# Chunk output of a selective scan: a seventh drive of sixteen by ScalarE and TensorE, the scaled input added by a diagonal matmul, the chunk written by ScalarE

## The reference

```
chunks = xn.reshape(B, L, 4, 64)...            # 4 chunks per batch item
h  = exp(dt*A[s]) * h + (dt*x)*B[s]            # for each of 16 states s, over 1024 tokens
y  = sum over s of h*C[s]  +  xc*D_param
ym = out_proj_w @ (y * silu(z))                # 128 -> 64 channels
ym = ym + skip_scale * chunks                  # what is called the skip below
```

## Time and profile before

| | us |
|---|---|
| median of 3 runs | 1836.05 (1835.17 to 1837.93) |
| the profiled execution | 1832.81 |
| its span, first to last instruction | 1830.9 |
| scans of the second item, gate of chunk 0 to the last read | 433.9 to 575.7 |
| mixture of experts, from | 1252.2 |

### The profile page before, as it was taken

One profiled execution on the slowest core, in us unless ns is written; L12 is line 12 of the kernel. 1 busy time (PEld: TensorE's weight loads), 2 busy tenths in 40 slices (PEclk: granted clock), 3 DMA queues, 4 the chain that ended last, 5 costly groups with the idle time before them and its releaser, 6 DMA issues. The chain is left out here.

```text
span 1830.9 us, 22984 instructions
## 1 busy us (share of the span) xinstructions
PE 1564.3 (85%) x6577; PEld 1012.4 (55%) x6578; DVE 1158.7 (63%) x1344; ACT 1002.1 (55%) x1950; POOL 1074.1 (59%) x574
## 2 busy tenths in 40 slices
PE   5589889979888888888898888673599999999997
PEld 2144435644444553443564444452488888888896
DVE  3399998489997579998758999746522222222222
ACT  6768775878874887885687877321122222222222
POOL 0499991279995158999037999300345555455543
PEclk9799999999999999999998999895699999999999
DMA  3356650156762055765026676642022222222222
GB/s 104 99 185 228 221 197 10 50 184 224 241 203 86 1 170 196 248 204 169 2 78 217 195 240 200 247 179 71 25 36 34 37 37 39 35 34 40 34 33 26
DMA packets 78401, 222.43 MB, mean 121 GB/s; under 512 B 12588, under 2 KB 31349, under 8 KB 74966
## 3 DMA queue, kind: packets, MB, share of 16 engines
q1 hardware_dynamic: 62390, 202.54, 32.8%
q0 software_dynamic: 15904, 18.66, 6.6%
HBM read 199.76 MB, written 19.82 MB: 120 GB/s over the span
## 5 line engine op out<-in xcount | busy, mean ns | idle before, releaser
L474 PE MATMUL psum<-HC_sb,ident_sb 128*128 128x512 f32 x768 | 368.4, 606 | 36.1 <-POOL HC_sb L1257 25.5
L1986 ACT ACTIVATE hgt_sb<-psum_moe,b_sb 128x256 f32<-128x256 f32 (+1 forms) x312 | 116.5, 456 | 379.8 <-PE psum_moe L1893 252.0
L474 PE MATMUL psum<-experts_sb 64*128 64x512 f32 (+5 forms) x834 | 258.4, 551 | 70.6 <-DVE HC_sb L1577 18.8
L1893 PE MATMUL psum_moe<-XGT_sb,w1s_sb 128*128 128x256 f32 (+1 forms) x1248 | 254.9, 363 | 0.0
L2138 DVE TENSOR_TENSOR YS_sb<-psum_moe,b_sb 128x256 f32<-128x256 f32 x71 | 30.1, 424 | 352.8 <-PE psum_moe L1893 349.2
L1893 PE MATMUL psum_moe<-experts_sb,hgt_sb 128*128 x1136 | 251.7, 379 | 0.7 <-DVE YS_sb L2138 0.7
L1870 POOL DMA_INDIRECT out<-YS_sb,scat_sb x71 | 128.3, 1806 | 209.5 <-DVE YS_sb L2142 193.1
L1138 ACT ACTIVATE psum<-experts_sb 128x1024 f32<-128x1024 f32 x168 | 186.1, 1108 | 118.2 <-DVE experts_sb L1567 70.5
L474 PEld LDWEIGHTS psum<-HC_sb,ident_sb 128*128 128x128 f32 x768 | 139.8, 191 | 189.3 <-issue 104.6
L1160 ACT ACTIVATE experts_sb<-experts_sb 128x128 f32<-128x128 f32 x704 | 227.7, 388 | 18.4 <-PE psum L477 15.2
L1893 PEld LDWEIGHTS psum_moe<-XGT_sb,w1s_sb 128*128 128x128 f32 x1248 | 219.5, 192 | 25.5
(11 more groups left out here) (298 smaller groups left out, 2381.0 us busy)
## 6 DMA issues: line engine op xcount, KB each, us to landing
X_XT_sb<-bc_rows SPq DMA_DIRECT2D x116, 512.0 KB, 4.1
DA_sb<-bc_rows SPq DMA_DIRECT2D x88, 512.0 KB, 5.2
experts_sb<-bc_rows SPq DMA_DIRECT2D x40, 512.0 KB, 5.4
SQ_sb<-bc_rows SPq DMA_DIRECT2D x40, 512.0 KB, 5.9
T_sb<-bc_rows SPq DMA_DIRECT2D x20, 512.0 KB, 5.5
experts_sb<-w1T SPq DMA_DIRECT2D x8, 1024.0 KB, 19.8
experts_sb<-w2T SPq DMA_DIRECT2D x8, 1024.0 KB, 21.8
X_sb<-x_tok SPq DMA_DIRECT2D x5, 1024.0 KB, 6.9
```

Source lines behind the costliest of these rows:

```text
L474: return nc.tensor.matmul(o, lhsT, rhs, start=start, stop=stop, **k)
L1893: return nc.tensor.matmul(o, lhsT, rhs, start=start, stop=stop, **k)
L1986: m = nc.scalar.activation(HGT[:, k, 4 * h + q, 0:w], psum[:, 2 * h + q // 2, (q % 2) * 2 * P:(q % 2) * 2 * P + w], ACT.Gelu, bias=b1[:, b ...
```

## The change

In the last three chunks of an item seven states instead of six are turned: 1, 4, 6, 8, 10, 12 and 14, where it was 1, 4, 6, 9, 12 and 14. So state 9 goes to GpSimd, and states 8 and 10 leave it. POOL_READS stays. For chunks 0, 1 and 2 the skip on VectorE is gone. The output projection now goes into the half of banks 4 and 5 that the C row used, half by half behind sum_states at s = 2 and s = 3, and each half gets a second matmul, which adds the scaled input by a diagonal of 64 x 64 (SKIP, made once at the start). ScalarE copies the sum to YM (chunk_out) at s = 5, behind its decay and blocks, and c_row of s = 5 waits for that. The decay of s = 3 doesn't wait for the chunk any more. The last chunk of an item is as it was.

```diff
-TURNED_DRIVES = ((6, 9, 12, 15),) + ((1, 4, 6, 9, 12, 14),) * (NC - 1)
+TURNED_DRIVES = ((6, 9, 12, 15),) + ((1, 4, 6, 8, 10, 12, 14),) * (NC - 1)
...
+        SKIP = FB[:, 0:DM]
... (TensorE, c_row)
+                    if c and s == 5:
+                        pe.wait_ge(ym_done, b * NC + c)
... (TensorE, out_proj)
-                def out_proj(c):
-                    i = min((c + 1) * NS + 1, NI - 1)
-                    pe.wait_ge(h_ready, b * NI + (i + 1))
-                    p0 = DM * (c % 2)
+                def out_proj(c, h):
+                    i, p0 = (c + 1) * NS + 1, DM * (c % 2)
+                    pe.wait_ge(yf_ready, b * NC + c + 1)
+                    pe.wait_ge(dve_read, b * dve_reads(NI) + dve_reads(i + 1))
+                    at = psum[p0:p0 + DM, 4 + h, :]
+                    mm(at, outp_w[:, :], YF[:, h * HL:(h + 1) * HL], True, False)
+                    m = mm(at, SKIP[p0:p0 + DM, :], xn[p0:p0 + DM, c // 2, h * HL:(h + 1) * HL], False, True)
+                    if h:
+                        m.then_inc(op_ready, 1)
... (TensorE, the loop over i)
-                    if i % NS == 1 and c:
-                        out_proj(c - 1)
...
                     sum_states(i - 1)
+                    if c and i % NS in (2, 3):
+                        out_proj(c - 1, i % NS - 2)
... (ScalarE, decay)
-                    if c and s == 3:
-                        act.wait_ge(ym_done, b * NC + c)
...
+                def chunk_out(c):
+                    act.wait_ge(op_ready, b * NC + c + 1)
+                    p0 = DM * (c % 2)
+                    nc.scalar.activation(halves(YM[p0:p0 + DM, c // 2, :]), crep[p0:p0 + DM, :, :], ACT.Copy).then_inc(ym_done, 1)
... (ScalarE, the loop over i)
                     scale_blocks(i)
+                    if i >= NS and i % NS == 5:
+                        chunk_out(i // NS - 1)
... (VectorE)
-                    if c and s == 2:
-                        skip(c - 1)
... (VectorE, start)
+            fold(v.tensor_tensor(SKIP, ident[:, 0:DM], ident[:, DM:P], ALU.add))
+            fold(v.tensor_scalar(SKIP, SKIP, scal[:, 0:1], None, ALU.mult))
```

More of the change, by code:

```diff
@@ L815, in sum_states, with last_out_proj @@
                     m.then_inc(ysum_done, 1)
-                def out_proj(c):
-                    i = min((c + 1) * NS + 1, NI - 1)
-                    pe.wait_ge(h_ready, b * NI + (i + 1))
-                    p0 = DM * (c % 2)
+                def out_proj(c, h):
+                    i, p0 = (c + 1) * NS + 1, DM * (c % 2)
+                    assert not on_pool(i) and all(on_pool(i + k) for k in (1, 2, 3)) and not on_pool(i + 4)
+                    pe.wait_ge(yf_ready, b * NC + c + 1)
[5 more added lines that the diff above has]
+                        m.then_inc(op_ready, 1)
+                def last_out_proj():
+                    c, p0 = NC - 1, DM * ((NC - 1) % 2)
+                    pe.wait_ge(h_ready, b * NI + NI)
                     for h in range(NH):
-                        if c == NC - 1 and h == 0:
+                        if h == 0:
                             pe.wait_ge(yf_half, b + 1)
@@ L825, in out_proj @@
                             pe.wait_ge(yf_ready, b * NC + c + 1)
[L826 to L829, removed]
+                        mm(psum[p0:p0 + DM, 2 + h, :], outp_w[:, :], YF[:, h * HL:(h + 1) * HL], True,
+                           True).then_inc(op_ready if h else op_half, 1)
                 pe.wait_ge(bc_spread, b * (3 * NC * 16) + 3 * NC * 16)
@@ L848, in scans @@
                 xhat_turn(b + 1, 0)
-                out_proj(NC - 1)
+                last_out_proj()
                 xhat_turn(b + 1, 1)
@@ L1605, in gate @@
                     v.tensor_tensor(halves(YF), ysum, halves(SZ[:, c, :]), ALU.mult).then_inc(yf_ready, 1)
[L1607 to L1612, removed]
                 for i in range(NI):
@@ L1692 @@
 PREP_EPS, PREP_DVE, PREP_ALL = 6, 11, 11 + 3 + 2 + 6 + 5 + 1
-FOLD_NBR, FOLD_WG, FOLD_DVE = 12, 14, 20
+FOLD_NBR, FOLD_WG, FOLD_DVE = 12, 14, 22
 FIRST_AT = 18
```

## The result

The changed kernel takes 1845.7 us in the median (1841.46 to 1850.34), the kernel before 1836.05. The ratio is 1.005, with a 95% interval of 1.0037 to 1.0064: slower by 9.65 us. The profiled execution is the one of 1845.7 us, with a span of 1843.9.

A forecast was written before the change was run, and what follows sets the result against it. GpSimd was taken to pace the tails, with VectorE close behind, and the output chain the heads. Heads +6.8 and tails -4.9 give +1.9 us per item, +7.6 on 1832.8, plus 3.2 to the median: 1843, range 1827 to 1857.

The forecast's parts named there:

- What bounds the kernel: GpSimd paces the tails, VectorE close behind; heads follow gate, output projection on TensorE, skip on VectorE, decay of s = 3.
- The chain in the head: From gate through TensorE's queue to ScalarE's copy at 13.3 us, then decay and scan of s = 6; heads +6.8 per item.
- The handover to TensorE: At the start of the head's chain: gate and handover to TensorE take 1.35 us.
- The changes of shape: On TensorE between gate and copy: changes of matmul shape cost 0.09 to 0.14 each, 0.5 us in the chain.
- The copy: ScalarE's copy of 64 x 1024 from PSUM, once per chunk: 1.02 us, as partitions don't count.
- The lower bound of 0.5: ScalarE's copy at 0.5 us if half the partitions were half the time; takes 6 us off, to 1837.
- The tails: From scan of s = 6 to the next gate: 0.2, 2.4 and 2.3 us come back in chunks 1 to 3, -4.9.
- that GpSimd can't run far ahead: In tails 2 and 3 GpSimd's reads wait for the late scan of s = 6, limiting work ahead; no separate size.
- The sum: Heads +6.8 and tails -4.9 give +1.9 us per item, +7.6 for four items.
- That the diagonal runs beside other work: Rival, faster: diagonal matmuls on TensorE cost next to nothing, heads lose some 2.0 us each; 1820 to 1827, chance 0.2.
- That all idle time comes back: Rival: VectorE's 7.5 us idle in the tails goes, against +6.8 for heads; 1833, near 1835, chance 0.2.
- That nothing comes back: Rival, slower still: heads add 6.8 us per item and tails return nothing; 1863, or 1853 with half; chance 0.15.

The follow-up runs named there:

- the two kernels with one half each: The kernel before with the seventh drive alone, 1815.95 us, ratio 0.9896; the changed kernel with the six old turned drives, 1851.45 us, ratio 1.0092.
- the one with equal shapes: The changed kernel with a 128 x 64 diagonal and the scaled input moved on all 128 rows: 1847.68 us, and 1845.37 us once more.
- the changed kernel's second run: The changed kernel once more, nothing changed, beside the kernel with the full-row diagonal on the same chip: 1846.34 us (1.0044 to 1.0072).

## Why the prediction was right

**What bounds the kernel.** GpSimd in the tails is shown for tails 2 and 3: relieving it alone shortens them by 2.25 and 2.08 and leaves every head at its place. In tail 1 GpSimd was busy throughout, but ScalarE stood so close behind that the relief was worth nothing. In the changed kernel's heads it is the output path: without the diagonals they are 2.0 shorter, with the copy behind the decay 1.1 to 1.55.

**The chain in the head.** This was the deciding step, and it held in its order and nearly in its sizes. The copy was put at 13.3 after the gate and starts at 453.66 - 440.16 = 13.50. The scan of s = 6 was put at 15.95, 15.65 and 15.55, and starts at 16.07, 15.84 and 15.70. The handover to TensorE was 0.1 shorter than I had (1.25 for 1.35), and the last matmul's end with the handover to ScalarE 0.15 shorter (0.11 behind 453.55, for 0.26). The changes of shape were under-sized, 0.5 forecast in the chain and 0.95 by the starts: 0.10 on the direct term, 0.09 going into the first half (445.82 to 447.63 is 1.81 for 1.72), 0.19 on the sum between the halves (1.91), and 0.29 and 0.28 over 1.72 in the halves. Part of the last 0.28 is the way out, which I had put behind the chain. Heads: +6.8 forecast, +7.2 measured. ScalarE still waits 0.89 us before the decay of s = 3, for the scan; I had said none, and it was 5.42.

**The copy.** 1019 ns for 64 x 1024, taken at 1.02. The lower bound of 0.5, half the time for half the partitions, is out.

**The tails.** 0.2, 2.4 and 2.3 forecast to come back, 0.01, 2.28 and 2.08 measured, in all 4.9 against 4.4. The mechanism had a part that I didn't see. In tail 3 either half of the change gives the 2.1 back by itself, the seventh drive or the head's own wait, as the two kernels with one half each show; my reason, one drive less, was enough but not needed, and that GpSimd can't run far ahead was wrong for this chunk. For chunk 2 it was right, by first_shift.

**The sum.** +1.9 per item forecast, +2.8 measured by the windows; end to end the four items give +10.9 and the medians +9.65, where 7.6 was the forecast. The terms that were mis-sized are the tails by 0.5 and the heads by 0.4 per item, both to the side of too fast. That the medians lie only 2 us above the forecast is in part luck: end to end it was 3.3. The Trainium skill, "TensorEngine Tiling (Array Packing)", section Key Properties, has a drain at each change of the tiling mode. The trace agrees in so far as changes of shape cost time, 0.29 over the matmuls in a half with its 64-row diagonal and 0.14 in the one with equal shapes.

**The rivals.** That the diagonal runs beside other work is refuted by its removal (2.0 us per head). That all idle time comes back is refuted by tail 1, which stayed at 33.65 with ScalarE at 32.90, and by the sum of 4.4 of 7.5. That nothing comes back is refuted by tails 2 and 3.

**The best version.** The seventh drive without the new output path, 1815.95 us, is 1% under the kernel before and 1.6% under the changed one.

## What to carry to other kernels

Two relieved loads don't add up when the wait that one of them brings already relieves the other; try each alone, and keep the one that pays. Whether an engine can use another's wait hangs on what stands in its own queue: one small operation that needs the late engine was enough to hold GpSimd up. Taking 1.2 us from the busiest engine is worth nothing if its result then needs a longer chain over two other engines before the next piece of work on that engine can start: count everything that stands in each queue between the release and that piece. An eviction put at a fixed place in an in-order queue holds up what is behind it for as long as its producer is late, so it belongs behind the next piece that somebody else waits for.

## What was not expected

The stretches outside the measured chunks differ by several microseconds between executions, though nothing in them was changed. The stretch from the first item's end to the second item's first gate, of the kernel before, and then of the changed kernel:

```profile
285.36:433.89 148.53, 131.04 (x580) 77.07 (x578) 112.03 (x174) 112.52 (x177) 65.89 (x28) 0.97 0.35 109
```

```profile
287.57:440.16 152.59, 137.91 (x582) 81.94 (x580) 109.99 (x174) 112.67 (x177) 64.92 (x28) 0.92 0.32 106
```

It is 4.1 us longer at a granted clock of 0.92 instead of 0.97, with TensorE busy 6.9 us more. In the profile of the changed kernel's second run it lasts 148.7 (from 289.19 to 437.92). The clock is not all of it: with the seventh drive alone the stretch behind the first item lasts 147.7 and the one behind the third 151.5, both at 0.97. So a few microseconds of any total arise in these stretches, and effects of 3 us have to be read from windows.

In the kernel with the later normalization TensorE waited 2.73 us for a late gate, and the ten records of projection, C row and direct term behind that gap took 5.80 us where they took 4.16 in the earlier trace rows. In the first item of the same profile they stood behind a wait of 2.64 us and took 4.16. First the second item, then the first:

```profile
525.25 5.80 PE L474 MATMUL psum<-experts_sb 128*64 128x512 f32 x10 [2.73 <-DVE experts_sb L1605]
```

```profile
237.57 4.16 PE L474 MATMUL psum<-experts_sb 128*64 128x512 f32 x10 [2.64 <-DVE experts_sb L1605]
```

From 525.25 to 530.89 the mean granted clock is 0.70, thus in part at the 1.2 GHz level, and 1.00 just before and after; in the first item it is 1.00 throughout. Items 3 and 4 are as the second, with a head of 14.44. So a late gate can cost 1.6 us more than its own lateness, and it need not. Why the clock fell behind the one wait and not behind the other, which is 0.09 us shorter, no run shows.
